# Two small layer-norm operations move from VectorE to GpSimd in a fused convolution, attention and mixture-of-experts kernel

## The reference

```
def _ln_t(v, eps=1e-05):
    m = jnp.mean(v, axis=-1, keepdims=True)
    s = jnp.var(v, axis=-1, keepdims=True)
    return (v - m) / jnp.sqrt(s + eps)

x = x + conv_attention(group_norm(x))            # per image
t = tokens of x                                   # 16 images x 256 tokens x 128 channels
t = t + attention(_ln_t(t))                       # 8 heads of 16, softmax, per image
t = t + experts(_ln_t(t))                         # router, best 2 of 8 experts per token
```

## Time and profile before

| | |
|---|---|
| time, median of 3 runs | 445.7 us (445.69 to 445.85) |
| the profiled execution's own time | 448.31 us |
| its span in the profile | 445.8 us |
| busy: PE, DVE, ACT, POOL | 365.0, 299.5, 261.3, 226.3 us |
| instructions of DVE and of POOL | 1075 and 317 |
| all of L919 and L920 on DVE (32 each) | 6.1 us and 5.2 us |
| all of L578 and L581 on POOL (32 each) | 22.6 us and 6.3 us |

### The profile page before, as it was taken

The page is one execution under the profiler, slowest core; times in us unless marked ns, Lnnn a source line. Parts: engine busy times, 40 slices in busy tenths (PEclk is TensorE's granted clock), DMA queues, the critical chain, the costliest instruction groups (busy, mean ns, idle before and its releaser), DMA issues.

```text
span 445.8 us, 9570 instructions
## 1 busy us (share of the span) xinstructions
PE 365.0 (82%) x2688; PEld 267.7 (60%) x2688; DVE 299.5 (67%) x1075; ACT 261.3 (59%) x662; POOL 226.3 (51%) x317
## 2 busy tenths in 40 slices
PE   1887878699888898988888785207999999999876
PEld 1353555466556665656555443105988888888776
DVE  5255567589999999999998955532455555555313
ACT  2254447588888888888875652103655566555404
POOL 5122213236666766666675654420667666666710
PEclk9999999899999999999998965557999999999969
DMA  8927428443433444332443000044233333321169
GB/s 248 308 84 203 109 77 288 108 109 88 124 90 99 132 133 119 99 98 85 133 132 97 26 27 24 25 140 122 63 82 93 96 97 89 93 75 48 51 227 350
DMA packets 43219, 52.28 MB, mean 117 GB/s; under 512 B 8208, under 2 KB 35760, under 8 KB 43024
## 3 DMA queue, kind: packets, MB, share of 16 engines
q1 hardware_dynamic: 38208, 40.97, 32.3%
q0 software_dynamic: 4544, 9.38, 6.4%
q10 hardware_dynamic: 416, 1.33, 1.0%
HBM read 33.70 MB, written 19.76 MB: 120 GB/s over the span
## 4 chain that ended last, share of the span: by engine, by line
DVE 30%; PE 22%; ACT 17%; issue 14%; DMA 6%; POOL 4%; SPq 3%; DVEq 2%; ACTq 1%; POOLq 0%
DVE gT L1087 6%; DVE mneg L905 5%; ACT rest L748 4%; PE PV L1153 3%; DVE yb L1095 3%; ACT ys L757 3%; ACT xT L741 2%; PE MX L1131 2%; DMA prob<-res 2%; PE W L1247 2%; PE W L1311 2%; DVE st L912 2%; ACT parts L656 2%; PE EX L1163 1%; PE W L1263 1%
## 5 line engine op out<-in xcount | busy, mean ns | idle before, releaser
L905 DVE TENSOR_REDUCE mneg<-MX 128x2 f32<-128x512 f32 x128 | 84.4, 678 | 7.0 <-PE MX L1131 6.4
L602 ACT ACTIVATE prob<-EX 128x512 f32<-128x512 f32 x128 | 70.9, 598 | 17.7 <-PE EX L1141 16.4
L527 POOL DMA_INDIRECT slots<-rows,dest x64 | 63.3, 989 | 20.3 <-issue 15.6
L1141 PE MATMUL EX<-qst,kst 99*128 99x256 bf16 x256 | 48.5, 287 | 8.4 <-ACT prob L602 4.9
L1131 PE MATMUL MX<-kst,qst 96*128 96x256 bf16 x256 | 49.3, 276 | 3.1 <-DVE mneg L905 3.1
L1384 PE MATMUL W<-w2s,gT 128*128 x312 | 42.7, 280 | 3.4 <-DVE yb L1095 1.8
L1384 PEld LDWEIGHTS W<-w2s,gT 128*128 128x128 f32 x312 | 38.6, 191 | 10.0 <-issue 8.6
L588 POOL DMA_INDIRECT res<-ys,xt x36 | 34.9, 969 | 17.5 <-ACT ys L757 12.0
L1374 PE MATMUL EX<-xT,Ae 128*128 128x256 f32 x156 | 41.0, 387 | 0.0
L1079 DVE COPY Ae<-A 128x512 f32 x39 | 16.6, 429 | 32.6 <-PE PV L1374 19.7
L1141 PEld LDWEIGHTS EX<-qst,kst 99*128 99x128 bf16 x256 | 21.9, 101 | 26.5 <-ACT prob L602 17.6
(11 more groups left out here) (190 smaller groups left out, 838.7 us busy)
## 6 DMA issues: line engine op xcount, KB each, us to landing
qk_parts<-parts SPq DMA_DIRECT2D x16, 384.0 KB, 2.8
qst<-qk_parts SPq DMA_DIRECT2D x16, 192.0 KB
kst<-qk_parts SPq DMA_DIRECT2D x16, 192.0 KB
xt<-slots SPq DMA_DIRECT2D x18, 130.0 KB, 2.1
qst<-qk_parts SPq DMA_DIRECT2D x16, 128.0 KB
kst<-qk_parts SPq DMA_DIRECT2D x16, 128.0 KB
X<-res SPq DMA_DIRECT2D x4, 512.0 KB, 6.7
prob<-res SPq DMA_DIRECT2D x4, 512.0 KB, 7.4
```

What stands on the lines that cost most here:

```text
L527: pool.indirect_dma_start(out=slots, out_offset=bass.IndirectOffsetOnAxis(ap=dest[q][:, n, k:k + 1], axis=0), in_=rows[q][:, n, k, :], in_ ...
L602: act.activation(prob[:, h, :, :], EX[h % 2][:], ACT.Exp, scale=SCALE).then_inc(s["ex_ok"], 1)
L905: dve.tensor_reduce(mneg[p][:, 2 * pair:2 * pair + 2, k], MX[c % 2][:], AX.X, ALU.max, negate=True).then_inc(s["mx_ok"], 1)
L1141: mm = pe.matmul(EX[h % 2][:, k, :], stack(kst, b, h, k * P, P, QROWS), stack(qst, b, h, rows=QROWS), start=True, stop=True)
```

## The change

Adding epsilon to the variance and negating the mean, two operations on 128 partitions by 2 numbers, leave DVE's `stats` and are made by POOL at the head of `root`, for both layer norms. POOL now waits for DVE's `agg` semaphore (both `bn_aggr` done) where it waited for `ve_ok`. The waits for `ve_ok` and `nm_ok` stay, now on POOL's own results.

```
             def root(b, q, ag, nm, ve, rs, nb, agg, nm_ok, ve_ok, rs_ok, nb_ok, used):

                 done(pool, s[used], b - 1, TPB)
+                done(pool, s[agg], b + 1, TPB)
+                pool.tensor_scalar(ve[q][:], ag[q][:, :, 1], LN_EPS, None, ALU.add).then_inc(s[ve_ok], 1)
+                pool.tensor_scalar(nm[q][:], ag[q][:, :, 0], -1.0, None, ALU.mult).then_inc(s[nm_ok], 1)
                 done(pool, s[ve_ok], b + 1)
                 pool.tensor_tensor(rs[q][:], ve[q][:], neg_half[:, 0:TPB], ALU.pow).then_inc(s[rs_ok], 1)
...
-            def stats(b, q, st, ag, ve, nm, ready, bn, agg, ve_ok, nm_ok, used, route):
+            def stats(b, q, st, ag, ready, bn, agg, used, route):
...
                     dve.bn_aggr(ag[q][:, k, :], st[q][:, k, :]).then_inc(s[agg], 1)
                 next(route, None)
-                done(dve, s[agg], b + 1, TPB)
-                dve.tensor_scalar(ve[q][:], ag[q][:, :, 1], LN_EPS, None, ALU.add).then_inc(s[ve_ok], 1)
-                dve.tensor_scalar(nm[q][:], ag[q][:, :, 0], -1.0, None, ALU.mult).then_inc(s[nm_ok], 1)
```

More of the change, by code:

```diff
@@ L568, in step, with root @@
                 if live(b):
-                    root(b, q, nm1, ve1, rs1, nb1, "nm1_ok", "ve1_ok", "rs1_ok", "nb1_ok", "tn1_ok")
+                    root(b, q, ag1, nm1, ve1, rs1, nb1, "agg1", "nm1_ok", "ve1_ok", "rs1_ok", "nb1_ok", "tn1_ok")
                 b, q = t - 5, o
                 if live(b):
-                    root(b, q, nm2, ve2, rs2, nb2, "nm2_ok", "ve2_ok", "rs2_ok", "nb2_ok", "tn2_ok")
-            def root(b, q, nm, ve, rs, nb, nm_ok, ve_ok, rs_ok, nb_ok, used):
+                    root(b, q, ag2, nm2, ve2, rs2, nb2, "agg2", "nm2_ok", "ve2_ok", "rs2_ok", "nb2_ok", "tn2_ok")
+            def root(b, q, ag, nm, ve, rs, nb, agg, nm_ok, ve_ok, rs_ok, nb_ok, used):
                 done(pool, s[used], b - 1, TPB)
+                done(pool, s[agg], b + 1, TPB)
+                pool.tensor_scalar(ve[q][:], ag[q][:, :, 1], LN_EPS, None, ALU.add).then_inc(s[ve_ok], 1)
+                pool.tensor_scalar(nm[q][:], ag[q][:, :, 0], -1.0, None, ALU.mult).then_inc(s[nm_ok], 1)
                 done(pool, s[ve_ok], b + 1)
@@ L1006, in step @@
                 if live(b):
-                    stats(b, q, st1, ag1, ve1, nm1, "T_ok", "bn1", "agg1", "ve1_ok", "nm1_ok", "nb1_ok", route)
+                    stats(b, q, st1, ag1, "T_ok", "bn1", "agg1", "nb1_ok", route)
                 b, q = t - 5, o
                 if live(b):
-                    stats(b, q, st2, ag2, ve2, nm2, "t2_ok", "bn2", "agg2", "ve2_ok", "nm2_ok", "nb2_ok", route)
+                    stats(b, q, st2, ag2, "t2_ok", "bn2", "agg2", "nb2_ok", route)
                 if t + 2 < len(GN):
```

## The result

The changed kernel is slower, by about 1%. Its median is 451.42 us (450.02 to 453.19, six runs) against 445.69 us (444.82 to 445.85, six runs) for the kernel before: ratio 1.0102, 95% interval 1.0071 to 1.0134. I had forecast 444.3 us and a range up to 446.6.

The account below looks back on a forecast made before the run. Two nearly equal chains, PE with ACT (13.04 us a step) and DVE, were taken to bound the kernel. Gains of 0.97 (full steps), 0.2 (behind step 15) and 0.25 (start) made 445.7 - 1.4 = 444.3 us, range 442.2 to 446.6.

Parts of the forecast that it names:

- two chains side by side: Full steps: PE and ACT take 13.04 us; DVE is just under it one step, 0.1 to 0.4 over the next.
- the short kind: Steps of 13.04 us from L1227 to L1227, where ACT's copy `mrow` decides; they alternate with longer ones where `cum` is late.
- DVE's saving: DVE loses 0.30 us a full step, worth something only where `cum` is late: 0.97 us over the full steps.
- that sign: Sign of a right forecast: L1227 always starts 0.39 to 0.40 us behind the start of `mrow`.
- x: Extra time of one POOL root from `ve` and `nm`: taken as 0.33 us, bounds 0.29 and 0.68.
- the room: `xnT` in front of PE's L1263: readable at 130.80 + 2x, wanted at 131.85, so free up to x = 0.52.
- rival three: POOL's second `nb` holds `xnT` before L1263; beyond x = 0.52 nine full steps each lose 2x - 1.05; 447.1 us; chance 0.12.
- my own formula: `xnT` can be read at 130.80 + 2x; beyond x = 0.52 each full step loses 2x - 1.05 us.
- the 1.4 gained: Forecast's whole gain in us: 0.97 in full steps, 0.2 behind step 15, 0.25 in the start.
- In step 2, and wherever POOL waits for the statistics: There POOL's `rs` was to come 0.10 to 0.17 us later; 0.12 was taken off the start's gain.

Follow-up runs that it names:

- dve_part: Changed kernel with `ve` and `nm` made nowhere, epsilon and the mean's sign left out of the result; 444.2 us against 448.03, ratio 0.9912.
- tt_forms: Changed kernel with POOL's two new operations as two-input operations against constant tiles; 445.95 us against 448.03 for the kernel before, ratio 0.9953.
- tt_mrow: tt_forms with ACT's copy `mrow` moved in front of `norm_plus_x`; ratio 0.9953, nine intervals 115.38 us.
- tt_double: tt_forms with each of POOL's two new operations made twice, copies into a tile nobody reads; ratio 1.0106, nine intervals 120.42 us.

## Why the prediction was wrong

**What held.** The two chains side by side, the copy `mrow` as the holder of the short kind, and DVE's saving as worth about 1 us in the loop: dve_part, tt_forms and tt_mrow show them. In step 0 `gstat` started 0.29 behind the start of `ag` (22.17 against 21.88) instead of 0.55, 0.26 saved where I had 0.18 to 0.25. Even after the change L1227 is 0.39 behind the start of `mrow`, as I had said it would be; but `mrow` is itself the end of a chain that POOL has made longer, and that sign alone proves nothing.

**The step that failed: the size of x, the time that POOL's two new operations add to a root.** "No row shows exactly them, so I bound one root's extra time x ... I take 0.33." It measured 0.62 (1.66 - 1.04 us for the first `nb`, 3.29 - 2.03 = 1.26 for both), inside the bound of 0.68. I took 0.15 us for an independent operation from `nb` to the next `rs`; both are of the two-input form, while `ve` and `nm` are not. The trace of before had this form on POOL, in two rows that stand between those of the earlier trace rows and that I had not weighed:

```profile
127.01 0.20 POOL L560 TENSOR_SCALAR mparts<-mrest 128x16 bf16<-128x16 f32 x1 [0.16 <-POOL mrest L558]
127.29 0.22 POOL L563 TENSOR_TENSOR mparts<-mrest,mparts 128x16 bf16<-128x16 f32 x1
```

Each reads the one in front, L560 the `mrest` that started at 126.63. The two-input L563 starts 0.28 behind the operation that it reads, the one-input L560 0.38 behind: the one-input form is 0.10 later for the same dependence. Twice that on my 0.33 would have been an estimate of 0.53, just past the edge that I had worked out myself.

**The second failure: the size of the room.** I wrote "POOL's longer row is free up to x = 0.52", that is, up to 1.05 us for both roots. The measured edge is 2.89 - 2.03 = 0.86 us, x = 0.43. The place was right: the last wait to end in front of L1263 is the one for `xnT`, as rival three says, with L1258's wait for `rows` just ahead of it. The profile puts 4.0 us of PE's idle time down to L1258 and almost none to L1263, because PE stands at L1258 first. Two steps of tt_mrow show the difference. Counted from their rank products, at 126.33 and 164.91, `rows` started 1.53 and 1.59 us behind, the transposition of `rows` 2.54 in both, the query projection 2.76 and 2.79, and the intervals were 12.79 and 12.84. Two terms were missing. From the end of `nb` to `rows` I took 0.08 us; it is 0.19. And I let PE's products follow each other as before once `xnT` is there; from L1263 to L1264 they take 0.08 more. 1.05 - 0.11 - 0.08 = 0.86. By my own formula the measured 1.26 us for both roots would have cost 0.21 a step, 1.9 us in nine, and with the 1.4 gained 446.2 us, inside my range. With the measured room it is 0.40 a step, 3.6 us.

**What wasn't counted.** I priced rival three in nine full steps alone, which gave 447.1 at worst. In step 16 PE no longer has the work that covered 2x, and 1.3 us were lost in that one interval, half of the nine intervals' net loss. In step 2, and wherever POOL waits for the statistics, I had 0.10 to 0.17 us; in step 0 `rs` starts 0.60 behind the end of `ag` (22.25 to 22.85) where it was 0.28.

So rival three was the right one, place and all. It had a chance of 0.12 only because x was put near its low end by rows of another form, and its price was too low because the room was put too wide. The Trainium skill ("GPSIMD Engine Reference", "Engine selection") speaks against elementwise work on GpSimd because two-input operations are about twice as slow there, and calls one-input operations roughly line-rate; here it was the two-input form that was cheap (0.15 us from start to start) and the one-input form that was not (0.31). For tiles of this size the measurement decides. The contention with VectorE at the shared interfaces that the Trainium skill states ("GPSIMD Engine Reference", "Specifications") does not show in `nb`, which takes 196 ns in the mean before and 195 after; no run varied DVE's work beside it, so the rule itself is not tested.

What stays open: where the 1.9 us are that loop and step 16 do not show, where in start and tail dve_part gains 2.7 us, and what decides how long the lower clock lasts around 80 us and behind 260 us.

## What to carry to other kernels

For small operations count from start to start and by form, not by duration; a busy share of 54% says nothing about a chain of eight starts one behind the other. When work moves to an engine with time to spare, follow its last result through every reader, and count at each the pick-up and what the next engine loses when it has to start again from a standstill. Then ask the same in the steps where the pipeline fills and empties, since the cover is gone there. If the move looks right and the time does not follow, try the other form of the same operation before undoing it.

## What the runs showed of the hardware

- On POOL a one-input operation with an immediate number (TENSOR_SCALAR, 128x2) started 0.28 to 0.31 us behind the operation in front though it needed nothing of it; a two-input one (TENSOR_TENSOR, 128x2) 0.15 to 0.18. Durations hide this: 0.22 to 0.23 against 0.19 to 0.20.
- The same operation of ACT picks up POOL's `nb` at different speed: `tn` started 0.09 us behind the end of its `nb` (130.57 to 130.66), `rows` 0.19 behind (132.21 to 132.40); in tt_double it was 0.08 and 0.18. In step 7 of after `rows` too started 0.09 behind (105.38 to 105.47). From step 8 on `rows` also waits until the rows of an earlier image are sent, and the chain of step 16 has two pieces of ACT's queue, 0.08 us apart (226.28 and 226.36), between `nb` and `rows`. The added wait goes with the added 0.1 us; no run took it out.
- PE did not only start later when it had stood for ACT: L1263 to L1264, same operands and size, took 0.52 us instead of 0.44, with L1263's weights loaded 0.02 instead of 0.10 us ahead.
- Executions of one unchanged kernel ranged from 443.9 to 450.9 us in three comparisons, while the sum of nine intervals of its loop was 117.96 and 117.97 us in two profiles.
